# Second layer's field: width differences from shifted copies instead of a product

## The reference, cut to what matters

```
def _L1_cond_ref(y, zX, zY, zR, dx, dy):                # y = x, (16, 256, 256): token, feature
    yp_x = pad(y, last axis by 1 on both sides, mode='reflect')
    lap_x = (yp_x[:, :, :-2] - 2.0 * y + yp_x[:, :, 2:]) / (dx * dx)    # along the features ("width")
    yp_y = pad(y, token axis by 1 on both sides, mode='reflect')
    lap_y = (yp_y[:, :-2, :] - 2.0 * y + yp_y[:, 2:, :]) / (dy * dy)    # along the tokens
    return zX * lap_x + zY * lap_y + zR * y * (1.0 - y)  # dx = dy = 1; zX, zY, zR: one number per batch
```

## Time and profile before

| | us |
|---|---|
| median of 3 runs | 2461.85 (2452.49 to 2463.63) |
| profiled execution | 2440.37 |
| its span, first to last instruction | 2438.6 |
| busy in the span: TensorE | 2262.9 (93%) |
| VectorE | 1840.2 (75%) |
| ScalarE | 1291.7 (53%) |
| GpSimd | 1005.2 (41%) |
| products with `lap`, 128 passes | 377 ns median, 634 at most |

### The profile page before, as it was taken

The page is one execution under the profiler, slowest core; times in us unless marked ns, Lnnn a source line. Parts: engine busy times, 40 slices in busy tenths (PEclk is TensorE's granted clock), DMA queues, the critical chain, the costliest instruction groups (busy, mean ns, idle before and its releaser), DMA issues.

```text
span 2438.6 us, 53844 instructions
## 1 busy us (share of the span) xinstructions
PE 2262.9 (93%) x18368; PEld 2057.9 (84%) x18368; DVE 1840.2 (75%) x5132; ACT 1291.7 (53%) x3839; POOL 1005.2 (41%) x1063
## 2 busy tenths in 40 slices
PE   4788989999887799999999999899999999999999
PEld 3677878778776688888888887799999999999999
DVE  5778787777878666666666665588868888888876
ACT  1666666666663455555555555434325555555522
POOL 5435445354444455555555554133322222222073
PEclk8999999999998899999999999899999999999999
DMA  4523323233240312212212113131226767777443
GB/s 138 177 87 102 107 88 109 86 99 107 82 129 3 82 38 56 51 44 56 50 45 57 47 47 85 28 79 36 45 73 226 233 229 234 237 230 236 146 121 124
DMA packets 196341, 259.23 MB, mean 106 GB/s; under 512 B 58646, under 2 KB 168486, under 8 KB 185318
## 3 DMA queue, kind: packets, MB, share of 16 engines
q1 hardware_dynamic: 187206, 237.13, 32.0%
q0 software_dynamic: 8864, 18.66, 3.0%
HBM read 176.10 MB, written 43.94 MB: 90 GB/s over the span
## 4 chain that ended last, share of the span: by engine, by line
PE 61%; DVE 15%; ACT 8%; POOL 7%; issue 6%; DMA 1%; POOLq 0%; SPq 0%; DVEq 0%; ACTq 0%
PE bank L55 51%; PE bank L136 6%; ACT Ph L654 2%; POOL P L1786 2%; ACT Ph L656 2%; PE bank L1296 1%; DVE Ph L815 1%; ACT PTh L666 1%; PE bank L1336 1%; DVE xe L921 1%; DVE sgs L945 1%; PE bank L399 1%; POOL Qn L1811 1%; POOL Qn L1809 1%; DVE hb L955 1%
## 5 line engine op out<-in xcount | busy, mean ns | idle before, releaser
L1490 ACT ACTIVATE P<-P,mx 128x144 f32<-128x144 f32 x512 | 206.2, 405 | 263.8 <-DVE mx L1611 262.9
L55 PE MATMUL bank<-xD_hi,w1e_lo 128*128 128x256 f32 x880 | 251.1, 285 | 0.0
L2623 POOL DMA_INDIRECT xE<-d_y,ixs x78 | 111.2, 1426 | 336.3 <-PE bank L136 300.8
L55 PE MATMUL bank<-w2e_hi,hrD_hi 128*128 128x256 f32 x880 | 249.0, 283 | 0.0
L55 PE MATMUL bank<-w2e_lo,hrD_hi 128*128 128x256 f32 x880 | 248.9, 283 | 0.0
L55 PE MATMUL bank<-w2e_hi,hrD_lo 128*128 128x256 f32 x880 | 248.9, 283 | 0.0
L1786 POOL TENSOR_TENSOR P<-P,rs 128x512 f32<-128x512 f32 x128 | 133.1, 1040 | 273.9 <-DVE rs L1620 270.4
L55 PE MATMUL bank<-xD_lo,w1e_hi 128*128 128x256 f32 x880 | 245.9, 279 | 0.0
L55 PE MATMUL bank<-xD_hi,w1e_hi 128*128 128x256 f32 x880 | 245.6, 279 | 0.0
L2232 ACT ACTIVATE hD<-bank,b1E 128x256 f32<-128x256 f32 x312 | 127.0, 473 | 197.2 <-PE bank L55 188.1
L1120 POOL TENSOR_TENSOR xe<-xe 128x704 f32<-128x704 f32 (+3 forms) x64 | 88.2, 1378 | 340.5 <-DVE xe L926 340.3
(11 more groups left out here) (324 smaller groups left out, 7922.3 us busy)
## 6 DMA issues: line engine op xcount, KB each, us to landing
w1raw<-in_ew SPq DMA_DIRECT2D x39, 1024.0 KB, 6.0
w2raw<-in_ew SPq DMA_DIRECT2D x39, 1024.0 KB, 4.9
stack<-d_rot SPq DMA_DIRECT2D x256, 96.0 KB, 2.7
K<-Kn SPq DMA_DIRECT2D x256, 72.0 KB, 2.1
d_rot<-QKh SPq DMA_DIRECT2D x64, 256.0 KB, 3.1
Q<-Qn SPq DMA_DIRECT2D x256, 64.0 KB, 2.0
d_ys<-oE SPq DMA_DIRECT2D x39, 256.0 KB, 2.6
d_rot<-QKl SPq DMA_DIRECT2D x32, 256.0 KB, 2.9
```

The lines of the kernel that those rows point to most:

```text
L55: inst = e.matmul(out, l, r, start=k == 0, stop=k == len(pairs) - 1)
L1490: inst = e.activation(P1[t % 2][:, n, :], P1[t % 2][:, n, :], ACT.Exp, bias=mx1[t % 2][:, 2 * g + sg:2 * g + sg + 1], scale=-1.0, accum_ou ...
L2623: e.indirect_dma_start(out=xE[q % 2][c], out_offset=None, in_=d_y, in_offset=bass.IndirectOffsetOnAxis(ap=ixs[r % 4][:, c:c + 1].bitcast(U ...
```

## The change

`laplace`, the matrix `lap` and its load are gone. SyncE instead copies batch b's features into two tiles, `near` (which takes the place of `lap`) and `fu`, shifted by one partition up and down: eight transfers within SBUF, of 112 and 15 partitions of 2 KB each and four single rows for the block borders and the reflected edges (`neighbours`). GpSimd adds the two into `near` in step 6 (`add_neighbours`; for batch 0 VectorE does it). The -2y of both directions moves into the per-batch scalar: `fa` now starts from zR - 2zX - 2zY instead of zR, so L1672 is gone. The last sum reads `near` in SBUF instead of PSUM. `project(b, 3)` no longer waits for the field, `category` of the last two batches no longer waits for the first field, and `differences` now waits for the add.

```diff
@@ pe_ab, category @@
-                    e.wait_ge(v_t7, 1)
+                    e.wait_ge(v_mul, 4 * b - 1)
@@ sync_c @@
+            def neighbours(b):
+                if not 0 <= b < B:
+                    return
+                y = X[:, b]
+                e.wait_ge(v_xf, b + 1)
+                if b:
+                    e.wait_ge(v_t7, b)
+                    e.wait_ge(v_rn, 2 * b)
+                for dst, src in ((near[1:113], y[0:112]), (near[113:128], y[112:127]),
+                                 (near[0:1, 1, :], y[127:128, 0, :]), (near[0:1, 0, :], y[1:2, 0, :]),
+                                 (fu[0:112], y[1:113]), (fu[112:127], y[113:128]),
+                                 (fu[127:128, 0, :], y[0:1, 1, :]), (fu[127:128, 1, :], y[126:127, 1, :])):
+                    e.dma_start(dst, src).then_inc(l_near, 16)
...
-            for dst, src in ((lap, "lap"), (gn, "gn"), (rot1, "rot1k")):
+            for dst, src in ((gn, "gn"), (rot1, "rot1k")):
...
+            neighbours(0)
             yield
...
             yield
+            neighbours(1)
             e.wait_ge(v_w1, 6)
...
                     stack(b, half)
+                    if half == 0:
+                        neighbours(b + 2)
@@ pe_c, project n == 3 @@
-                    if b + 1 < B:
-                        e.wait_ge(v_t7, b + 2)
-                    else:
-                        e.wait_ge(v_x1r, 8 * b + 1)
+                    e.wait_ge(v_x1r, 8 * b + 1)
@@ pe_c: laplace and its calls @@
-            def laplace(b):
-...
-                    if b == -3 and s == 0:
-                        laplace(0)
-                    if s == 1:
-                        laplace(entering(b))
@@ dve_c @@
                 else:
-                    e.wait_ge(s_v, vs.n)
+                    e.wait_ge(l_near, LNEAR + 128)
+                    e.tensor_tensor(near, near, fu, ALU.add).then_inc(g_near, 1)
+                e.wait_ge(g_near, b + 1)
+                e.wait_ge(s_v, vs.n)
                 e.tensor_scalar(fa, y, zN, zR, ALU.mult, ALU.add).then_inc(*vs.up())
...
-                e.scalar_tensor_tensor(out=fu, in0=y, scalar=-2.0, in1=fu, op0=ALU.mult, op1=ALU.add).then_inc(*vs.up())
...
-                e.wait_ge(p_lap, b + 1)
-                e.scalar_tensor_tensor(out=fa, in0=lap_bank(b), scalar=zX, in1=fa, op0=ALU.mult, op1=ALU.add
+                e.scalar_tensor_tensor(out=fa, in0=near, scalar=zX, in1=fa, op0=ALU.mult, op1=ALU.add
                                        ).then_inc(v_t7, 1)
...
+            for i in range(2):
+                e.wait_ge(s_v, vs.n)
+                e.scalar_tensor_tensor(out=zs[:, 2, :], in0=zs[:, i, :], scalar=-2.0, in1=zs[:, 2, :], op0=ALU.mult,
+                                       op1=ALU.add).then_inc(*vs.up())
@@ pool_c @@
+            def add_neighbours(b):
+                if not 0 < b < B:
+                    return
+                e.wait_ge(l_near, LNEAR + 128 * (b + 1))
+                e.tensor_tensor(near, near, fu, ALU.add).then_inc(g_near, 1)
+                e.wait_ge(g_near, b + 1)
...
                         combine(b + 1, 7)
+                        add_neighbours(entering(b + 1))
```

More of the change, by code:

```diff
@@ L1186, in program @@
         tile("space0", 32)
-        lap, rot1 = tile("lap", 2, 256), tile("rot1", 3, 256)
+        near, rot1 = tile("near", 2, 256), tile("rot1", 3, 256)
         fa, fu, rn1 = tile("fa", 2, 256), tile("fu", 2, 256), tile("rn1", 256)
@@ L1213, in program @@
         l_st, LST = [[l_x[0], l_x[1]], [l_x[2], l_wa]], [[16, 16], [16, 128]]
-        p_S1, p_T1, p_PV1, p_qk1, p_V1, p_lap, p_one, p_back = (sem(f"p_{n}") for n in (
-            "S1", "T1", "PV1", "qk1", "V1", "lap", "one", "back"))
+        p_S1, p_T1, p_PV1, p_qk1, p_V1, p_one, p_back = (sem(f"p_{n}") for n in (
+            "S1", "T1", "PV1", "qk1", "V1", "one", "back"))
+        g_near = sem("g_near")
+        l_near, LNEAR = l_rw, 96 * B
         v_mx1, v_ri1, v_PT1, v_O1, v_t7, v_rn, v_xn, v_x1r, v_back, v_w1 = (sem(f"v_{n}") for n in (
@@ L1230, in entering @@
             return b + 2 if b >= -1 else B
-        def lap_bank(b):
-            return halves(0 if b else 5)
         def sums_bank(b):
@@ L1722, in split_back @@
                                 wo1[0][:, f:f + 2, :].bitcast(F32), ALU.subtract).then_inc(v_w1, 1)
-            e.wait_ge(l_c, 96)
+            e.wait_ge(l_c, 80)
             e.tensor_scalar(zs[:, 3, :], zs[:, 2, :], -1.0, None, ALU.mult).then_inc(*vs.up())
+            for i in range(2):
+                e.wait_ge(s_v, vs.n)
+                e.scalar_tensor_tensor(out=zs[:, 2, :], in0=zs[:, i, :], scalar=-2.0, in1=zs[:, 2, :], op0=ALU.mult,
+                                       op1=ALU.add).then_inc(*vs.up())
             for b in range(-3, B + 1):
@@ L1911, in program @@
         WE = WD + 3
-        LD, LW, LP, LO = 96, 32, 32, 16
+        LD, LW, LP, LO = 80, 32, 32, 16
         ZEROED, READY = 3, 4
@@ L2733 @@
     A["w_gate"], A["w_up"], A["w_down"] = g["L0_ffn_w_gate"], g["L0_ffn_w_up"], g["L0_ffn_w_down"]
-    lap = np.zeros((256, 256), np.float32)
-    for w in range(256):
-        lap[w, w] -= 2.0
-        lap[w, 1 if w == 0 else w - 1] += 1.0
-        lap[w, 254 if w == 255 else w + 1] += 1.0
-    A["lap"] = T2(np.ascontiguousarray(lap.T))
     A["gn"] = g["L1_attn_g_norm"].reshape(2, 128).T
```

## The result

The changed kernel took 2477.38 us (median of five executions, 2473.31 to 2479.79), the kernel before 2457.89 (median of five, 2452.49 to 2463.63). The ratio is 1.0074, with a 95% interval of 1.0052 to 1.0096: slower by 0.79% of the medians, 19.5 us, where I had forecast 7.1 us and 2469. The time lies inside the range; the change itself is nearly three times what I had forecast. The profiled execution of the changed kernel took 2479.78 (span 2477.7).

What follows compares the result with a forecast made beforehand. It took each period as bound by TensorE from step 7's turn to step 3, then a latency chain through VectorE and GpSimd. 17.8 - 8.5 - 2.2 = +7.1 us on the 2461.85 median gave 2469 us, range 2449 to 2483.

Steps and rivals of the forecast that it cites:

- The sum on the chain: Second layer's period: GpSimd's add in step 6, ahead of `normal` of step 7, costs 1.37 us, 13 times, 17.8 us.
- The product: Second layer's period: of the removed `lap` product's 1.92 us only 0.43 comes through at the turn of step 1.
- gain 0.61, not 0.98: At the turn of step 2: TensorE allows 0.98 us, but L1671 beside GpSimd leaves 0.61; times 14, 8.5 us.
- TensorE as the bound: Rival for the period: the add hides and the step 1 stall closes, 34 us less, 2428; chance 0.10.
- a falling clock: Rival for the period: granted clock falls behind a new TensorE stall, 33 us above the forecast, 2502; chance 0.08.
- late transfers: Rival: copies take over 9 us from issue, each us beyond costs 13 us; chance 0.04.
- The join: Where the second layer's first steps are woven into the first layer's last: -2.2 us in all, allowed -8 to +4.
- gains of 0.5: At the join: first `lap` product, 3.31 us at half clock, goes; VectorE is late next, so 0.5 us gained.
- 2.1 (L1672): At the join: L1672 is on the chain with 2.08 us, and its removal gains 2.1 us.
- I take half of the 3.8 as lost: At the join: `differences(1)` starts 3.8 us later, waiting for GpSimd's add; L1661 then runs alone, so 1.9 us lost.
- The third batch's loss of 0.7: At the join: its transfers go out behind `stack(0, 0)` just as GpSimd needs them, about 0.7 us lost.
- The gain of 2.2: At the join, 798.93: TensorE's 5.53 us wait for L1683 goes; `turn_hidden`, next held by L1135, starts 2.2 us earlier.

Runs made afterwards that it cites:

- x2: Kernel before plus one more 128x512 GpSimd sum at the end of step 6 for 13 batches, into an unread tile; 2464.62 us, ratio 1.0040.
- x4: Changed kernel with GpSimd's sum over only 4 of 256 columns, transfers, waits and order kept; 2458.42 us, ratio 0.9998 to the kernel before.
- x3: Kernel before without the product with `lap`; L1672 stays, VectorE's last field step reads a tile in SBUF; 2462.02 us, ratio 1.0013.
- x10: Changed kernel with four more transfers of the same sizes per batch, from the fourth batch on; 2475.26 us, ratio 1.0082 to the kernel before.
- x13: Changed kernel with GpSimd's sum behind step 7's normalization, the second batch's sum on VectorE, and the product's instructions back on 8 columns; 2438.28 us, ratio 0.9993.
- x12: Changed kernel with GpSimd's sum behind step 7's normalization and the second batch's sum on VectorE; 2439.98 us, ratio 0.9999 to the kernel before.
- x5: Changed kernel with GpSimd's sum moved from the end of step 6 to behind step 7's normalization; 2454.67 us, ratio 0.999 to the kernel before.
- x8: Changed kernel with the second batch's sum on VectorE ahead of its differences, not on GpSimd; 2469.55 us in one execution.
- x11: Changed kernel with the product's 8 instructions per batch put back on 8 columns, result unread; 2463.94 us, ratio 1.0098 to the kernel before.

## Why the prediction was right, and where it was wrong

**The sum on the chain** (17.8 us, 1.37 a period): right. 1.37 in the chain, 1.39 by adding the sum alone (x2), 1.18 by thinning it (x4).

**The product** (0.43 of 1.92 us come through to step 1): right at that turn, 10.09 against 10.52 us in x3. That step 2 would take it back was part of the forecast (gain 0.61, not 0.98, for VectorE and GpSimd in each other's way); x3 showed it with 0.04 us for the product alone. The mean period rose by 0.81, forecast 0.76, and the part from first to last `x_low` by 10.6 us against 9.3. The rivals on TensorE as the bound, on a falling clock and on late transfers are out: a stall of 1.33 and one of 1.47 us, clock 1.00 in the period, x10.

**The transfers**: free, as said. They are issued from 1237.11 to 1242.56 and land in 1.7 to 2.6 us (medians by size; 3.3 at the longest), and the sum starts at 1250.95 (1204.36 and one period of 46.59), over 5 us behind the last landing.

**The join** (-2.2 us, with -8 to +4 allowed): wrong, it is about +5.8 and 1 more ahead of it, outside its own bounds. Two steps failed. The first is the gains of 0.5 ("The first product with `lap` is on the chain at half clock") and 2.1 (L1672). The forecast took them at the clock of the kernel before; in the changed kernel the clock of 710 to 730 us is 0.74 for 1.00, and 2.0 us are lost up to the wait. x13, at 0.99, has them (22.9 us to the earlier L985 for 25.3). The rival that the clock falls was priced for the period and not for the join. The second is "I take half of the 3.8 as lost". The wait was forecast at 3.8 and is 3.83, and L1661 behind it does take 0.55 for 1.51, but 2.6 (x12 against x5) to 3.1 (x8) came through. The third batch's loss of 0.7 is a wait of 1.29 and lies behind the stretch. The gain of 2.2 has no run of its own; x3, which has the product's part of all gains, is no shorter at the join than the kernel before.

**Behind the layer** (not in the sum): about 4 us by timed runs, 9.5 by profiles, and open how much of it the usual executions of the kernel before have too. The forecast said that a change of 7.1 "carries over as it is"; it had no term for a part of the program that both kernels share. The measured terms give 10.6 + 5.8 + 1 + 4 = 21.4, against 19.5 timed (12.8 to 23.6 by the interval of the ratio).

That the total still fell into the range is partly luck: two errors of one sign, 9 and 4 us, inside bounds that had been drawn for other terms. And the base, 2461.85 as the median of three, was 4 us above the 2457.89 of five, so that 2469 is nearer to the result than 7.1 is to 19.5.

## What to carry to other kernels

In a kernel whose period is a chain through several engines, ask where in its engine's queue a new instruction stands before asking how long it is: the same sum cost 1.4 us a period ahead of the normalization that the next turn needs, and nothing behind it. Work taken from the busiest engine (93% here) is worth only what the next engine in the chain lets through, and that may be given back one step later, as 0.43 us was here. At a place where two phases interweave, look at the granted clock first: a gain read at full clock was gone at 0.74. And count a wait in full until a row shows its cover.

## What was not expected of the hardware

- VectorE's `scalar_tensor_tensor` over 128x512 with both inputs in SBUF took 0.75 us with GpSimd idle and 2.05 beside it (803.21 after); a `tensor_tensor` 0.69 and 1.78 (771.57 in x8).
- A stall of TensorE, VectorE and ScalarE for up to about 10 us (x3), in code that no edit touched, came with ten of ten profiles of kernels without the full product, and at most in small part in the four others. Its cause is open. Putting the number of TensorE's instructions back did not remove it.
- The same code of the join ran at a granted clock of 0.70 to 1.00 in 710 to 730 us, 1.00 in four of four profiles with the full product; one edit, the short passes, came with 0.70 (x11) and 0.99 (x13). Eight passes took 3.37 us at the low clock and 1.74 at the high one.
- One program has different medians on different chips: 2458.08, 2456.97 and 2440.65 us for the kernel before. A difference of 10 us needs both kernels on one chip.
